# Layer 3's sums in three pairs of PSUM banks instead of two, with the own scores in one bank and the carry chain's small results in the bank of the turned scores

## The reference

```python
def _gat_conv(x, src, dst, W, a_src, a_dst, bias, heads, out_ch, n_nodes):
    h = (x @ W).reshape(n_nodes, heads, out_ch)
    alpha_s = jnp.einsum('nhc,hc->nh', h, a_src)
    alpha_d = jnp.einsum('nhc,hc->nh', h, a_dst)
    e = jax.nn.leaky_relu(alpha_s[src] + alpha_d[dst], negative_slope=0.2)
    m = jax.ops.segment_max(e, dst, num_segments=n_nodes)
    ex = jnp.exp(e - m[dst])
    denom = jax.ops.segment_sum(ex, dst, num_segments=n_nodes)
    a = ex / (denom[dst] + 1e-16)
    msg = h[src] * a[:, :, None]
    out = jax.ops.segment_sum(msg, dst, num_segments=n_nodes)
...
    out1 = _gat_conv(x_norm, src, dst, W1, a_src1, a_dst1, b1, H1, C1, n)
    out2 = _gat_conv(x_norm, src, dst, W2, a_src2, a_dst2, b2, H2, C2, n)
    x_cat = jax.nn.elu(jnp.concatenate([out1, out2], axis=-1))
    unified = x_cat @ Wu + bu
    return residual + unified
```

## Time and profile before

| | |
|---|---|
| median of 3 runs | 4878.01 us (4874.4 to 4884.42) |
| the profiled execution's own time | 4869.96 us |
| its span, first to last instruction | 4868.2 us |
| granted TensorE clock, mean | 0.712 |
| busy: PE, DVE, ACT, POOL | 3104.0, 3152.1, 2250.4, 2855.3 us |
| layer 3's sums in the trace | 3870 to 4762 us |

### The profile page before, as it was taken

How to read it: one execution, slowest core, us unless ns; L and a number is a source line. 1 busy time by engine, 2 the same in 40 slices (tenths; PEclk the granted TensorE clock), 3 DMA queues, 4 the chain that set the end, 5 groups by cost and what they waited for, 6 DMA issues and landing times. The chain is left out here.

```text
span 4868.2 us, 74715 instructions
## 1 busy us (share of the span) xinstructions
PE 3104.0 (64%) x14124; PEld 2235.3 (46%) x14204; DVE 3152.1 (65%) x10653; ACT 2250.4 (46%) x8908; POOL 2855.3 (59%) x2739
## 2 busy tenths in 40 slices
PE   1577875777623666645777773566662677777776
PEld 0366664656422444433545542344431355555554
DVE  5887775666454555574767764666664577777776
ACT  0355554555422333334666663333334355555454
POOL 0377776777706777724777752777750465555522
PEclk9855556555556777766666676767775799898899
DMA  1000000000024444424555532444440666666531
GB/s 50 1 2 2 2 2 2 2 2 2 2 56 135 128 133 132 127 35 118 139 143 139 144 86 87 132 132 121 131 79 13 213 187 173 173 173 171 167 92 61
DMA packets 235833, 449.02 MB, mean 92 GB/s; under 512 B 80264, under 2 KB 132390, under 8 KB 235110
## 3 DMA queue, kind: packets, MB, share of 16 engines
q0 software_dynamic: 130816, 317.16, 25.2%
q1 hardware_dynamic: 104752, 128.89, 8.1%
HBM read 416.04 MB, written 29.80 MB: 92 GB/s over the span
## 5 line engine op out<-in xcount | busy, mean ns | idle before, releaser
L1237 POOL DMA_INDIRECT rows.4<-feats,by_dst_other.1 x464 | 511.5, 1102 | 564.8 <-issue 342.1
L1237 POOL DMA_INDIRECT rows.2<-feats,by_dst_other.1 x464 | 494.5, 1066 | 279.6 <-POOLq L976 138.5
L1237 POOL DMA_INDIRECT rows.1<-feats,by_dst_other.1 x464 | 490.8, 1058 | 280.5 <-POOLq L976 139.4
L1237 POOL DMA_INDIRECT rows.3<-feats,by_src_other.1 x448 | 475.5, 1061 | 255.8 <-issue 128.3
L658 POOL DMA_INDIRECT by_dst_records<-r_rec.1,r_idx.1 x448 | 443.2, 989 | 161.1 <-issue 127.9
L658 POOL DMA_INDIRECT by_src_records<-r_rec.2,r_idx.2 x416 | 413.5, 994 | 143.7 <-issue 112.3
L1445 ACT ACTIVATE rows.4<-rows.4,xres.1 128x65 f32<-128x65 f32 x1856 | 448.0, 335 | 0.9
L1364 PE MATMUL m_p.4<-rows.4,xres.1 128*128 128x264 f32 x1044 | 324.0, 438 | 145.7 <-DVE acc.4 L1613 109.8
L1445 ACT ACTIVATE rows.2<-rows.2,e_prob.2 128x33 f32<-128x33 f32 x1856 | 397.9, 315 | 0.0
L1613 DVE TENSOR_TENSOR acc.4<-acc.4,m_p.4 128x264 f32 x522 | 200.4, 425 | 219.3 <-PE m_p.4 L1381 183.6
L1345 PE MATMUL m_p.3<-rows.3,m_oh.3 128*128 128x260 f32 x896 | 309.2, 497 | 16.4 <-DVE rows.3 L1594 15.5
(11 more groups left out here) (761 smaller groups left out, 8230.6 us busy)
## 6 DMA issues: line engine op xcount, KB each, us to landing
e_line.1<-by_dst_own_row SPq DMA_DIRECT2D x29, 512.0 KB, 4.7
e_line.2<-by_dst_own_row SPq DMA_DIRECT2D x29, 512.0 KB, 4.4
e_line.4<-by_dst_own_row SPq DMA_DIRECT2D x58, 256.0 KB, 5.0
e_line.3<-by_src_own_row SPq DMA_DIRECT2D x28, 512.0 KB, 4.6
xres.1<-by_dst_masks SPq DMA_DIRECT2D x232, 48.0 KB
e_mask.2<-by_dst_masks SPq DMA_DIRECT2D x29, 320.0 KB
rows.1<-feats,by_dst_other.1 POOLq DMA_INDIRECT x464
rows.2<-feats,by_dst_other.1 POOLq DMA_INDIRECT x464
```

The source lines that it names most:

```text
L1237: pool.indirect_dma_start(out=rows[:, s % RING, :], out_offset=None, in_=feats, in_offset=bass.IndirectOffsetOnAxis(ap=g.other[:, s:s + 1] ...
```

## The change

In layer 3 (NC = 2) alone: BANKS goes from 2 to 3, so an opening waits for the group three before, and in one wait ahead of both convolutions. For the banks, e_po shrinks to one (32 words a slot): the first two parts of the own score are written side by side (24 columns) and a second matmul adds the third part onto the second, and VectorE reduces over two instead of three. The results of turn_ends, turn_carry and the factor go to the last columns of e_pt's bank. Since ScalarE and VectorE would then read one bank, the factor waits for "shifted" instead of "carry_read". The add of a group becomes one VectorE instruction over both banks, and a closing signals once. With NC = 1 the same instructions come out as before.

```diff
-    BANKS = 4 // NC
+    BANKS = 4 if NC == 1 else 3
+    PARTS = 3 if NC == 1 else 2
...
-        pcar = ps("e_pc", [P, 512], F32, c2)
         BACK = FOLDS * P
         LASTS = BACK + CS * HS
-        CARRY = 2 * CS
-        FACT = 4 * CS
+        if NC == 1:
+            pcar, ENDS, CARRY, FACT = ps("e_pc", [P, 512], F32, c2), 0, 2 * CS, 4 * CS
+        else:
+            pcar, ENDS, CARRY, FACT = pturn, LASTS, LASTS, LASTS + 2 * CS
...
-                    ins = pe.matmul(po[:, s - s0, 0:3 * HS], hot[:, hh % 2, i * P:(i + 1) * P],
-                                    parts[:, :, bass.ds(ids[s % 4], 1), :].rearrange("p k a h -> p k (a h)"), start=True, stop=True)
+                    own_hot = hot[:, hh % 2, i * P:(i + 1) * P]
+                    ins = pe.matmul(po[:, s - s0, 0:PARTS * HS], own_hot,
+                                    parts[:, 0:PARTS, bass.ds(ids[s % 4], 1), :].rearrange("p k a h -> p k (a h)"), start=True, stop=PARTS == 3)
+                    if PARTS == 2:
+                        ins = pe.matmul(po[:, s - s0, HS:2 * HS], own_hot,
+                                        parts[:, 2, bass.ds(ids[s % 4], 1), :].rearrange("p a h -> p (a h)"), start=False, stop=True)
...
                 scaled(s)
+                if group >= BANKS:
+                    pe.wait_ge(S["added"].sem, S["added"].at(group_added(group - BANKS)))
                 for k in range(NC):
-                    if group >= BANKS:
-                        pe.wait_ge(S["added"].sem, S["added"].at(group_added(group - BANKS) - NC + 1 + k))
...
                 for k in range(NC):
-                    pe.matmul(pp[:, group % BANKS, k, 0:1], zeros[:, :], zeros[:, 0:1], start=False, stop=True).then_inc(S["closed"].sem, 1)
+                    ins = pe.matmul(pp[:, group % BANKS, k, 0:1], zeros[:, :], zeros[:, 0:1], start=False, stop=True)
+                ins.then_inc(S["closed"].sem, 1)
...
-                act.wait_ge(S["carry_read"].sem, S["carry_read"].at(c + 1))
+                if NC == 1:
+                    act.wait_ge(S["carry_read"].sem, S["carry_read"].at(c + 1))
+                else:
+                    act.wait_ge(S["shifted"].sem, S["shifted"].at(c + 1))
...
-                dve.tensor_reduce(e, po[:, 0:m, 0:3 * HS].rearrange("p s (k h) -> p s h k", k=3), X, ALU.add).then_inc(S["own_summed"].sem, 1)
+                dve.tensor_reduce(e, po[:, 0:m, 0:PARTS * HS].rearrange("p s (k h) -> p s h k", k=PARTS), X, ALU.add).then_inc(S["own_summed"].sem, 1)
...
-                for k in range(NC):
-                    a = acc[:, bass.ds(tile, 1), k * AW:(k + 1) * AW].rearrange("p a f -> p (a f)")
-                    dve.tensor_tensor(a, a, pp[:, group % BANKS, k, 0:AW], ALU.add).then_inc(S["added"].sem, 1)
+                a = acc[:, bass.ds(tile, 1), :].rearrange("p a (k f) -> p (a k) f", k=NC)
+                dve.tensor_tensor(a, a, pp[:, group % BANKS, :, 0:AW], ALU.add).then_inc(S["added"].sem, 1)
```

More of the change, by code:

```diff
@@ L1119, in stream_edges @@
     NCH, NG = len(chunks), SLOTS // 4
-    STEP = 512 * FOLDS // CS
+    STEP = 512 // CS
     BY_ACT = (1, 3) if NC == 1 else ()
-    BANKS = 4 // NC
+    BANKS = 4 if NC == 1 else 3
+    PARTS = 3 if NC == 1 else 2
     PAIRS = g.paired
@@ L1162, in group_added @@
     def group_added(k):
-        return (k + 1 + k // (CS // 2 + 1)) * NC
+        return k + 1 + (k // (CS // 2 + 1)) * NC
     def halves(c):
@@ L1313, in turn_ends @@
                 pe.wait_ge(S["topped"].sem, S["topped"].at(c + 1))
-                pe.matmul(pcar[0:HS, 0:2 * CS], of_head[0:R, :], spread[0:R, :, :, :].rearrange("p f d s -> p (f d s)"),
+                pe.matmul(pcar[0:HS, ENDS:ENDS + 2 * CS], of_head[0:R, :], spread[0:R, :, :, :].rearrange("p f d s -> p (f d s)"),
                           start=True, stop=True).then_inc(S["ends_out"].sem, 1)
@@ L1533, in carries @@
                 link(dve.tensor_copy(end[:, :, 1:CS + 1].rearrange("h d (f s) -> h f d s", f=FOLDS),
-                                     pcar[0:HS, 0:2 * CS].rearrange("h (f d s) -> h f d s", f=FOLDS, d=2)))
+                                     pcar[0:HS, ENDS:ENDS + 2 * CS].rearrange("h (f d s) -> h f d s", f=FOLDS, d=2)))
                 link(dve.tensor_tensor_scan(run[:, 1, 0:m + 1], join[:, par, 0, 0:m + 1], end[:, 1, 0:m + 1], LOWEST, ALU.add, ALU.max))
@@ L1607, in add_group @@
                 group = group0(c) + k
-                dve.wait_ge(S["closed"].sem, S["closed"].at(NC * (group + 1)))
+                dve.wait_ge(S["closed"].sem, S["closed"].at(group + 1))
                 if group:
                     dve.wait_ge(S["added"].sem, S["added"].at(group_added(group - 1) + (NC if k == 0 else 0)))
-                for k in range(NC):
-                    a = acc[:, bass.ds(tile, 1), k * AW:(k + 1) * AW].rearrange("p a f -> p (a f)")
-                    dve.tensor_tensor(a, a, pp[:, group % BANKS, k, 0:AW], ALU.add).then_inc(S["added"].sem, 1)
+                a = acc[:, bass.ds(tile, 1), :].rearrange("p a (k f) -> p (a k) f", k=NC)
+                dve.tensor_tensor(a, a, pp[:, group % BANKS, :, 0:AW], ALU.add).then_inc(S["added"].sem, 1)
             steps_of = (score, largest, carries, shift)
@@ L1671, in stream_edges @@
                       messages_too=SLOTS if NC == 2 else NG * len(BY_ACT), slot_sums=SLOTS,
-                      closed=(SLOTS // 2 + NCH) * NC if PAIRS else 0,
-                      added=(SLOTS // 2 + NCH) * NC + (NCH - 1) * NC if PAIRS else SLOTS + (NCH - 1) * NC, row_gate=NG - RB)
+                      closed=SLOTS // 2 + NCH if PAIRS else 0, added=(SLOTS // 2 + NCH if PAIRS else SLOTS) + (NCH - 1) * NC, row_gate=NG - RB)
         for name in ("own_summed", "scored", "turned", "topped", "ends_out", "carried", "carry_out", "carry_read", "rescale", "shifted", "exps",
```

## The result

The changed kernel takes **4838.8 us** (median of 4 runs, 4830.18 to 4839.46) against 4878.85 for the kernel before: ratio 0.992, 95% interval [0.9907, 0.9933]. That is 40 us faster, where 4877 was forecast with a range of 4838 to 4918. The profiled execution took 4839.27 us, its span is 4837.5.

A forecast was written before the change was run, and what follows sets the result against it. No engine was full: PE and DVE alternate in layer 3, with 109.8 us of PE waits for adds removable. Chunks +2.4, last two chunks -7.0, layer start +3.6 gave -1.0 us: 4877 us from 4878.01, range 4838 to 4918 (8 in 10).

The forecast's parts named there:

- sum of a chunk: Layer 3's sums: 10 chunks at -0.4 us and 16 at +0.4 us, together +2.4 us.
- the first kind: Chunks with mean clock 0.94 in layer 3's sums: +0.5 - 0.4 - 0.5 = -0.4 us each.
- Wait for the add: Start of a chunk, behind turn_ends: group 3's opening no longer waits for an add, -1.02 us.
- the second picks: Eight picks behind group 4's closing: cost nothing, as PE's sequencer prepares them ahead; rival that they aren't hidden: 4908 us, chance 0.11.
- Own scores: Second matmul per pick, 0.20 us each: first eight picks of a chunk exposed, +1.6 us.
- Add: VectorE's add of a group as one instruction: 0.07 us saved each, -0.3 us a chunk where DVE is last.
- Factor: Between group 4's add and turn_back: the factor's ACTIVATE now precedes the exponential, +0.2 us, between 0 and 0.4.
- Reduction: VectorE's reduction shrinks from 576 to 384 columns: 0.2 us off 0.75, always on the path.
- the second kind of chunk: Chunks with mean clock 0.89, where group 4's opening falls into the half-speed stretch: +1.0 - 0.1 - 0.5 = +0.4 us.
- the clock falls for longer: Rival, at the first picks: one more slow stretch and longer idle before turn_scores, +36 us, 4913 us; chance 0.17.
- Last two chunks: End of layer 3's sums, without picks: waits for adds go, -5.3 us in the last, -1.7 before it, together -7.0.
- Start of the layer: 32 picks stand alone, +6.4 us, partly covered by DVE's 2.78 us wait for gathered rows: +3.6 us.

## Why the prediction was off by 38 us

The measured time lies inside the range, 0.8 us from its lower end, and the likeliest case was wrong in size: a gain of 40 us where 1 was summed. The step that failed is the **sum of a chunk**: forecast +0.1 us on the mean (+2.4 over 26), measured -1.20. Two parts of it failed in opposite directions. At full clock a chunk shrank by some 2.5 us (26.8 after 29.3 to 29.5), where the first kind was given -0.4. And the slow stretches, whose mix was left as it was, take 4.0 us in 19 of 26 chunks. That the sum of both stayed within the range is partly luck. By its terms:

- *Wait for the add.* That PE's 109.8 us would fall to under 20 was right (2.0). That this number is the most the third pair can take away was wrong: with the price of the picks in place the pair is worth 123 us. I had put the second picks at nothing, rightly where PE works at half speed, but only as a cost that doesn't arise. In the kernel before they were exposed, at issue pace (4.31 us between the openings of groups 5 and 6), because the wait stopped the sequencer, and taking the wait away also wins that back. PE's weight loads for the sums waited 122.3 us for "issue" before and 26.3 after. A wait's own idle time doesn't contain what is queued behind it on the sequencer.
- *Own scores.* +1.6 us for the first eight: measured 1.1, as 0.14 each. The register operation was taken from the first matmul's 118 ns; it is 57. The row of the joinings had 57 to 146 and could have been the lower bound. PE's idle "issue" around the picks did not grow by 1.6 us a chunk, as was to show it; it fell from 52 to 36 us in all, since the second matmuls fill it as busy time. By the Trainium skill's 25 ns (TensorE: Matmul & The Clock Gate, Wait — 56ns, not 53.3ns?) the eight would have cost 0.2 us. The trace agrees with it where the sequencer is ahead (16 matmuls within 0.40 us, 4078.90 to 4079.30), and not at these eight, whose pace is the sequencer's.
- *Add.* 703 ns was worked out as 702. The shorter add was put at -0.3 a chunk; splitting it again costs 0.69 on the mean, of which 0.3 to 0.4 in chunks of one kind.
- *Factor.* +0.2: nearly nothing, since it overlaps the exponential.
- *Reduction.* 0.55 us instead of 0.75, as forecast.
- *Clock.* I put the second kind of chunk at +0.4 and let the mix stand. It didn't: the clock's mean fell to 0.87, outside the 0.88 to 0.92 that I had named, and yet the time fell. Of the 26 chunks four have no slow stretch and take 26.8 us; two have one at the start alone, where PE has waited 2.03 us for the scores, and take 27.7 and 27.8; one has one behind the picks alone and takes 29.5; the other 19 have both and take 30.2 to 31.5. The rival "the clock falls for longer" was right that the idle time ahead of turn_scores would grow (1.62 to 2.03) and that there would be one slow stretch more. The clock that was to decide it was just reached (0.87), and yet the rival's sign was wrong for the whole, because it had nothing won at full clock. What decides whether a chunk's clock falls is open: all 26 have 2.02 to 2.04 us of idle time there.
- *Last two chunks.* -5.3 for the last: measured -5.2. -1.7 for the one before: nothing (25.50 after 25.58 us), since it now ran a stretch at half speed (0.87 in the window 4690 to 4716).
- *Start of the layer.* +3.6. The first sum came 3.3 us later after acc's clearing (38.7 against 35.4), but the first rescale came 1.5 earlier. The kernel before waited for gathered rows once more than the 2.78 us that I had subtracted (1.14, at 3853.73), and behind the 2.78 it ran two openings at half speed (1.97 and 2.10 us) where the changed kernel has one of 1.63 and one of 1.14.

The picks (0.5), the factor (0.2) and the add (0.1 at most) make up 0.8 us of the 2.1 by which a chunk at full clock shrank more than was forecast. The rest, by elimination, is the released sequencer and what follows from it; no run prices it alone.

The rule of the Trainium skill on cycling through banks (TensorE: Matmul & The Clock Gate, A second HAM failure mode: psum-queue depth-cycling), that short idle gaps between groups of matmuls make the clock oscillate and that this costs throughput, agrees with the trace: the clock goes from 1.00 in one chunk to 0.84 in the next, its mean fell from 0.90 to 0.87, and a chunk with slow stretches in both places takes 4.0 us more than one without. The kernel as a whole became faster all the same.

## What to carry to other kernels

A wait on an in-order engine also stops the sequencer that prepares what stands behind it (read here from start times and from what the weight loads waited for); price a removed wait by the next stretch at issue pace, and not only by its own idle time. Where the clock changes between stretches of one kind, compare stretches with the same clock before you explain a mean: here it told 0.3 to 0.4 us of an add from 0.3 us of clock. Small matmuls with computed addresses cost by the sequencer and by the clock behind them, so spread them into places where TensorE waits anyway, before giving it more banks: here the spreading alone brought 86 us and the third pair with all that it needs 40, and both together 156 (4875.8 to 4719.3). Whether an add of two banks should be one instruction or two depends on whether the other engine waits for half of it: with two pairs one instruction cost 0.35%, with three it gained 0.3%, part of it by the clock.

## What the runs showed of the hardware that was not expected

- 432 added matmuls of 512 columns made the kernel 27 us faster, since TensorE stayed at 2.4 GHz behind the picks (clock 0.97 after 0.87).
- The length of an idle time did not decide TensorE's clock: behind 2.02 to 2.04 us of it ahead of turn_scores the next opening ran at half speed in 21 of 26 chunks of the changed kernel and at full speed in 5. At the same place in the kernel before, with 0.91 to 1.97 us (mostly 1.62), it never did.
- Prepared ahead by the sequencer, 16 small matmuls with computed addresses started within 0.40 us; at the sequencer's pace they start 0.13 to 0.22 us apart.
- A register operation ahead of a matmul took 57 ns when the address came from the index that the matmul before had used, and 121 for the first.
- ScalarE started an exponential 0.08 us after a small ACTIVATE of 0.18 us: put one behind the other they cost less than their sum.
